# Attention with its two layer normalisations moved from DVE to ACT, and DVE's small work laid out anew

## The reference, cut to what matters

```python
x = x + attention(layernorm(x), ctx)        # x, ctx: (16, 128, 256); 16 heads of 16, causal mask
x = x + ffn(layernorm(x))                   # 256 -> 1024 -> gelu -> 256, block floating point

def layernorm(x):                           # per row of 256
    return (x - mean(x)) / sqrt(var(x) + 1e-5)

def block_quant(v):                         # input of both ffn products, blocks of 32
    e = floor(log2(max(abs(block))))
    return round(block / 2**(e - 3)) * 2**(e - 3)
```

## Time and profile before

| | us |
|---|---|
| median of 3 runs | 251.42 |
| the runs | 248.55 to 251.74 |
| the profiled execution | 250.06 |
| its span, first to last instruction | 248.1 |
| PE, DVE, ACT, POOL busy | 213.2, 205.4, 174.5, 119.4 |

### The profile page before, as it was taken

How to read it: one execution, slowest core, us unless ns; L and a number is a source line. 1 busy time by engine, 2 the same in 40 slices (tenths; PEclk the granted TensorE clock), 3 DMA queues, 4 the chain that set the end, 5 groups by cost and what they waited for, 6 DMA issues and landing times.

```text
span 248.1 us, 6413 instructions
## 1 busy us (share of the span) xinstructions
PE 213.2 (86%) x2072; PEld 158.0 (64%) x2072; DVE 205.4 (83%) x880; ACT 174.5 (70%) x458; POOL 119.4 (48%) x120
## 2 busy tenths in 40 slices
PE   7894997997999979999999999778759849959974
PEld 7673775776776757777777777555327526735753
DVE  4443489899499999899999989897696999999971
ACT  2335887978887867987987998774634734856872
POOL 2610015343962954614524432522634757868892
PEclk9998999998899999999999999988976998997999
DMA  6593662743344243234234234387503102010212
GB/s 210 138 297 64 193 166 48 258 85 68 90 88 81 81 96 75 67 77 96 47 81 85 53 68 96 65 134 133 88 16 74 42 21 60 29 42 24 63 50 80
DMA packets 46576, 22.49 MB, mean 91 GB/s; under 512 B 21700, under 2 KB 46288, under 8 KB 46544
## 3 DMA queue, kind: packets, MB, share of 16 engines
q1 hardware_dynamic: 43472, 19.27, 34.2%
q10 hardware_dynamic: 3072, 2.82, 3.8%
HBM read 7.61 MB, written 2.11 MB: 39 GB/s over the span
## 4 chain that ended last, share of the span: by engine, by line
PE 37%; DVE 27%; SPq 16%; issue 9%; DMA 5%; ACT 2%; POOL 2%; ACTq 1%; DVEq 0%
PE bank L1021 8%; DVE prob L782 7%; SPq L257 4%; SPq L287 4%; PE bank L1128 4%; DVE probT L791 4%; SPq L250 4%; PE s_banks L1192 4%; PE s_banks L1070 4%; PE bank L1222 3%; PE bank L1109 3%; PE s_banks L1086 3%; DMA w_rows<-in_L_xattn_Wq 3%; DVE bank L943 2%; DVE hrn L957 2%
## 5 line engine op out<-in xcount | busy, mean ns | idle before, releaser
L457 ACT ACTIVATE prob<-prob,negm 128x128 f32<-128x128 f32 x256 | 81.0, 390 | 19.0 <-DVE negm L782 18.9
L782 DVE CUSTOM_DVE_ANT_0 prob<-s_banks,mask_f 128x128 f32<-128x128 f32 x256 | 58.8, 286 | 12.6 <-PE s_banks L1070 12.5
L683 POOL TENSOR_TENSOR hq<-hrn,h_mag 128x1024 bf16<-128x1024 f32 (+1 forms) x17 | 31.1, 1832 | 19.0 <-DVE hrn L957 16.4
L1021 PE MATMUL bank<-cT,wT 128*128 128x256 f32 x128 | 33.1, 406 | 0.0
L1070 PE MATMUL s_banks<-KS,QC 16*128 16x128 f32 x512 | 23.3, 296 | 8.7 <-DVE QC L771 3.8
L1070 PEld LDWEIGHTS s_banks<-KS,QC 16*128 16x128 f32 x512 | 17.3, 185 | 17.9 <-issue 16.3
L1021 PEld LDWEIGHTS bank<-cT,wT 128*128 128x128 f32 x128 | 25.5, 210 | 3.3
L517 ACT ACTIVATE s_banks<-s_banks 128x512 f32<-128x512 f32 x32 | 17.8, 580 | 10.3 <-PE s_banks L1192 10.1
L583 POOL TENSOR_TENSOR XQ<-xr,x_mag 128x512 bf16<-128x512 f32 x8 | 8.4, 1048 | 33.9 <-DVE xr L860 33.9
L1086 PE MATMUL s_banks<-ident_f,prob 128*128 128x128 f32 x124 | 20.2, 288 | 4.9 <-DVE negm L782 4.0
L1109 PE MATMUL bank<-probT,V 128*32 128x128 f32 x512 | 20.6, 279 | 3.1 <-DVE probT L791 3.0
(11 more groups left out here) (116 smaller groups left out, 430.2 us busy)
## 6 DMA issues: line engine op xcount, KB each, us to landing
oden<-oT SPq DMA_DIRECT2D x60, 64.0 KB, 2.4
KS<-full SPq DMA_DIRECT2D x32, 64.0 KB, 2.3
VS<-full SPq DMA_DIRECT2D x64, 32.0 KB, 2.0
QS<-full SPq DMA_DIRECT2D x29, 64.0 KB, 2.3
out<-full SPq DMA_DIRECT2D x14, 128.0 KB, 1.7
X<-in_x ACTq DMA_DIRECT2D x1, 1536.0 KB, 7.8
cbuf<-in_ctx SPq DMA_DIRECT2D x6, 256.0 KB, 4.6
fc_rows<-in_L_ffn_w_fc SPq DMA_DIRECT2D x1, 1024.0 KB, 6.1
```

The lines of the kernel that those rows point to most:

```text
L457: ins = nc.scalar.activation(prob[:, k % 4, u, s, :], prob[:, k % 4, u, s, :], ACT.Exp, bias=negm[:, k % 4, u, s:s + 1], scale=-1.0)
L683: nc.gpsimd.tensor_tensor(blocks(hq[par][:, some]), blocks(hrn[par][:, some]), spread(h_mag[par][:, n * nb:(n + 1) * nb], nb), ALU.subtract)\
L782: V.tensor_tensor_reduce(prob[:, k % 4, u, s, :], s_banks[:, 2 * (k % 2) + u, s * P:(s + 1) * P], mask_f[:, :], 1.0, LARGEST, ALU.add, ALU ...
L1021: ins = T.matmul(proj_bank(p, t)[:, c * PT:(c + 1) * PT], wT[:, t, k, c, :], src[:, k, :], start=(k == 0), stop=(k == KC - 1))
```

## The change

The six calls of `norm1` for pairs 2 to 7 and the normalisation of pairs 0 to 4 in `quantise` are done by ACT, as an activation with scale rs and bias -mean * rs, both one value per row. POOL makes that bias: two more operations of 128x2 in each of these `power1` and `power2`. On DVE `stats1` moves from group 2 to group 1, the block maxima from group 1 to group 2, `quantise_rest` from group 2 to group 3. On POOL `round_rows` moves behind `power1` and `queries_apart`. Pairs 0 and 1 of the first, and 5 to 7 of the second normalisation stay on DVE. Left out of the diff below are four new tiles of 128x2 (less1, off_1, less2, off_2) and the semaphores less_1, less_2, shift1 and shift2.

```diff
@@ -477,6 +481,21 @@
                                out_b[:, :].rearrange("p (k j r) -> p j k r", j=NJ, r=RPH))\
                     .then_inc(sm["o_copied"], 1)
 
+            def norm1(p):
+                act.wait_ge(sm["shift1"], p - 1)
+                act.wait_ge(sm["tx_done"], p)
+                for b in range(2):
+                    nc.scalar.activation(xn[:, b, :], X[:, 2 * p + b, :], ACT.Identity, scale=rs1[:, b:b + 1],
+                                         bias=off_1[:, b:b + 1]).then_inc(sm["xn_ready"], 1)
+
+            def norm2(p):
+                act.wait_ge(sm["shift2"], p + 1)
+                if p:
+                    act.wait_ge(sm["round2"], p)
+                for b in range(2):
+                    nc.scalar.activation(xn2[:, b, :], X[:, 2 * p + b, :], ACT.Identity, scale=rs2[:, b:b + 1],
+                                         bias=off_2[:, b:b + 1]).then_inc(sm["xn2_done"], 1)
+
             def step(i, par, first, last):
                 k = 2 * NW * i
                 exps(k)
@@ -492,6 +511,8 @@
                 copy_v(i, par)
                 if not last:
                     copy_proj(i + 1, 1)
+                if i > 2:
+                    norm2(i - 3)
 
                 exps(k + 4)
                 exps(k + 5)
@@ -505,6 +526,7 @@
                 copy_out(i, 0)
                 if ahead(i):
                     copy_tc(i + 2)
+                    norm1(i + 2)
                 if not first and not last:
                     invert(i - 1)
 
@@ -571,11 +593,25 @@
             def power1(p):
 
                 pool.wait_ge(sm["eps1"], p + 1)
+                if p > 1:
+                    nc.gpsimd.tensor_scalar(less1[:, :], mv1[:, :, 0], -1.0, 0.0, ALU.mult, ALU.add)\
+                        .then_inc(sm["less_1"], 1)
                 nc.gpsimd.tensor_tensor(rs1[:, :], ve1[:, :], neg_half[:, :], ALU.pow).then_inc(sm["pow1"], 1)
+                if p > 1:
+                    pool.wait_ge(sm["less_1"], p - 1)
+                    pool.wait_ge(sm["pow1"], p + 1)
+                    nc.gpsimd.tensor_tensor(off_1[:, :], less1[:, :], rs1[:, :], ALU.mult).then_inc(sm["shift1"], 1)
 
             def power2(p):
                 pool.wait_ge(sm["eps2"], p + 1)
+                if p < NPAIR - 3:
+                    nc.gpsimd.tensor_scalar(less2[:, :], mv2[:, :, 0], -1.0, 0.0, ALU.mult, ALU.add)\
+                        .then_inc(sm["less_2"], 1)
                 nc.gpsimd.tensor_tensor(rs2[:, :], ve2[:, :], neg_half[:, :], ALU.pow).then_inc(sm["pow2"], 1)
+                if p < NPAIR - 3:
+                    pool.wait_ge(sm["less_2"], p + 1)
+                    pool.wait_ge(sm["pow2"], p + 1)
+                    nc.gpsimd.tensor_tensor(off_2[:, :], less2[:, :], rs2[:, :], ALU.mult).then_inc(sm["shift2"], 1)
 
             def round_rows(p):
 
@@ -635,13 +671,13 @@
                 if 1 <= i < 4:
                     for u in range(3 * i - 3, min(3 * i, 8)):
                         round_weights(u)
-                if i > 2:
-                    round_rows(i - 3)
                 if ahead(i):
                     power1(i + 2)
                 if not last:
                     queries_apart(i + 1, 1 - par)
-                else:
+                if i > 2:
+                    round_rows(i - 3)
+                if last:
                     normalise(i - 1)
                     power2(i - 2)
 
@@ -835,10 +871,11 @@
 
             def quantise(p):
 
-                dve.wait_ge(sm["pow2"], p + 1)
+                if p >= NPAIR - 3:
+                    dve.wait_ge(sm["pow2"], p + 1)
                 if p >= NPAIR - 2:
                     dve.wait_ge(sm["h_exp_done"], 4 if p == NPAIR - 2 else LAST_OUT + 4)
-                for b in range(2):
+                for b in range(2 if p >= NPAIR - 3 else 0):
                     V.tensor_scalar(normal2(p)[:, b * E:(b + 1) * E], X[:, bass.ds(2 * p + b, 1), :].rearrange("p o e -> p (o e)"),
                                     mv2[:, b, 0:1], rs2[:, b:b + 1], ALU.subtract, ALU.mult)\
                         .then_inc(sm["xn2_done"], 1)
@@ -902,8 +939,8 @@
                 copy_pt(k)
                 maxes(k + 3)
                 copy_pt(k + 1)
-                if i > 2:
-                    quantise(i - 3)
+                if ahead(i):
+                    stats1(i + 2)
                 weights_at(i, 1)
 
                 maxes(k + 4)
@@ -911,9 +948,7 @@
                 maxes(k + 5)
                 copy_pt(k + 3)
                 if i > 2:
-                    quantise_rest(i - 3)
-                if ahead(i):
-                    stats1(i + 2)
+                    quantise(i - 3)
                 weights_at(i, 2)
 
                 if last:
@@ -922,8 +957,8 @@
                 copy_pt(k + 4)
                 maxes(k + 7)
                 copy_pt(k + 5)
-                if ahead(i):
-                    norm1(i + 2)
+                if i > 2:
+                    quantise_rest(i - 3)
                 weights_at(i, 3)
                 if last:
                     stats2(i - 2)
```

More of the change, by code:

```diff
@@ L88, in build_program @@
         rs1 = sb("rs1", [P, 2])
+        less1 = sb("less1", [P, 2])
+        off_1 = sb("off_1", [P, 2])
         xn = sb("xn", [P, 2, E])
@@ L117, in build_program @@
         rs2 = sb("rs2", [P, 2])
+        less2 = sb("less2", [P, 2])
+        off_2 = sb("off_2", [P, 2])
         xn2 = sb("xn2", [P, 2, E])
@@ L142, in build_program @@
         names = """x0_in x1_in x_in c0_in c1_in wq_in wk_in wv_in wp_in bias_in brow_in fc_in pj_in
-            iota v1_set qs_set warm perm_set row_cast col_cast row_bits wT_in wT_out wp_permuted b_parts b_moved ones_set
+            iota v1_set qs_set warm perm_set row_cast col_cast row_bits wT_in wT_out wp_permuted b_parts b_moved ones_set less_1 less_2 shift1 shift2
             bpart_set bn1 ag1 eps1 pow1 xn_ready tx_done tx_copied tc_done tc_copied
```

## The result

The changed kernel takes **254.62 us** (median of 4 runs, 252.23 to 257.98) beside 250.42 us for the kernel before on the same chip (4 runs, 248.55 to 251.74); the ratio is 1.0156, 95% interval 1.009 to 1.0221. Timed again with the second group of experiments it is 1.016 (1.0069 to 1.0251). That is slower by more than nothing; that it is slower by less than 2% is likelier than not but not shown, since both intervals reach past 1.02. Ratios here compare undisturbed runs only and medians are over all runs, so a quotient of two medians can differ from the ratio beside it.

A forecast was written before the change was run, and what follows sets the result against it. PE, DVE's extra work and the loop of SP and ACT were taken as near-equal bounds. Terms 1.28 + 3.38 = 4.7 us gave 254.7 on the profile, 256.1 on the median; forecast 255.4 us, range 251.5 to 259.

The forecast's parts named there:

- slower, by less than 2%: Whole kernel: forecast 255.4 us, a sum just under the 2% (5.0 us) line; chance within 2% 0.52.
- The loop of SP and ACT: SP's transfers and ACT's copy_out: turn grows to 19.83 us, KS issues at 85.41, 105.24, 125.07 and 144.90.
- The pair's price: ACT's normalising pair from SBUF, scale and bias per row: 0.80 us taken, 0.72 and 1.28 kept as ends.
- The gain of steps 3 and 4: DVE's work removed: 1.6 us back in step 3, at most 0.5 us a step over steps 4 to 6.
- The sum, its first term: Step 7 begins 1.63 us late by the copy of QS, 0.35 taken back on DVE: 1.28 us.
- The sum, its second term: Last step: late rounding moves normalise(6) on POOL from 172.88 to 176.26; all 3.38 us goes to the end.
- The statistics in group 1 ...: nothing, at most 0.2: Steps 1 and 2: statistics beside an exponent group of the weights, third group lighter by as much; at most 0.2 us.
- The dear pair: Rival: pair on ACT costs 1.28 us instead of 0.80; sum 6.6 us, 258.0 on the median; chance 0.28.
- The shorter queue: Rival: SP's part of a turn about 12.2 us, turn 18.9, nothing accumulates; sum 1.8 us, 252.5; chance 0.13.
- Not slower: Rival: ACT absorbs the pair, steps 4 to 6 run at PE's 18.38 us; 250.0 to 251.3; chance 0.06.
- The signs: KS issues near 105, 125, 145; PE waiting for xn, steps 4 to 6; DVE's wait before quantise(5) 2 us longer.

The follow-up runs named there:

- Experiments 2: Changed kernel with ACT's norm1 pair ahead of copy_out(i, 0) instead of behind copy_tc; 1.0027 against the kernel before, 250.79 us beside 251.04.
- experiment 5: Changed kernel with two buffers for oT used in turn, norm1 left in place; 1.0027 against the kernel before, 250.25 us beside 251.07.
- experiment 8: Kernel before with two buffers for oT, nothing else; ratio 1.0023, 250.36 us beside 251.57.
- experiment 4: Kernel before with only quantise_rest(4) moved behind the last maxima and copies on DVE; ratio 1.0096, 253.59 us beside 251.04.
- experiment 1: Changed kernel with POOL's normalise(6) and power2(5) ahead of round_rows(4) in the last step; 1.0155 against the kernel before, 253.99 us beside 251.04.
- experiment 10: Changed kernel with two oT buffers, POOL's normalise(6) and power2(5) ahead of round_rows(4), and first three steps' statistics in group 2; 0.9951 against the kernel before, 248.82 us.
- 9: Changed kernel with two oT buffers and POOL's normalise(6) and power2(5) ahead of round_rows(4); 0.9973 against the kernel before, 249.16 us beside 251.57.

## Why the forecast was right, and where it was not

The forecast was 255.4 us, and 254.62 came; "slower, by less than 2%" was the likeliest case, and the measured 1.0156 lies in it, though the interval reaches 1.022. That the change is slower, and by the loop, was foreseen; that the size fits so well is luck, because in the profile both terms of the sum came out otherwise.

**The loop of SP and ACT: right.** KS issues were forecast at 85.41, 105.24, 125.07 and 144.90 and came at 85.77, 104.80, 124.43 and 144.41. Experiments 2 and 5 open the loop in two different ways, and each brings 1.016 to 1.003. PE waits 0.74 us for ACT before the transposes of `xn` in steps 5 and 6, and these steps are 19.6, where 19.8 was forecast. That the loop was as near to being the bound as PE in the kernel before is not borne out: opening it there shows no gain (experiment 8).

**The pair's price: too low.** Taken at 0.80 us from a pair out of PSUM with one bias, measured 0.98 to 0.99. From the Trainium skill (ScalarE: Activation LUTs, What ACT_TABLE_LOAD costs) I had estimated 0.98, and the trace now agrees with it. The near row differs in two things, one operand per row in place of two and PSUM in place of SBUF; no run here separates them.

**The gain of steps 3 and 4: right in kind, larger.** Forecast were 1.6 us in step 3 and up to 0.5 in each steady step; step 3 went from 20.84 to 18.26 and step 4 from 18.87 to 18.26. So the loop bound only from step 5 on, not from step 4.

**The sum, its first term: 1.28 forecast, 0.05 measured.** The forecast let step 7 begin late, by the copy of QS. Step 7 began at 155.74, where it had begun at 155.69. QS was issued 1.14 us later, but its transfers landed 2.4 to 2.7 us after their issue, where one had taken 3.8 before, and POOL's copy began at 154.60 for 154.55; and steps 3 and 4 had won more than was forecast. What the loop costs in step 7 is seen beside experiment 5, where step 7 begins 3.88 us earlier and the rounding comes 1.94 earlier.

**The sum, its second term: 3.38 forecast, 2.11 measured.** `normalise(6)` began at 174.99, where 176.26 was forecast. The chain of the rounding was priced rightly: the add 0.41 after the copies, POOL 0.77 after that, free 1.00 later for 1.15. But the copies let go of DVE at 172.81, not at 173.93, the time taken over from the kernel before. There PE's project of pair 5 (four matmuls of 128x256, twice) took 1.92 and 1.09 us, at a granted clock of 0.58 from 166 to 170; in the changed kernel it took 1.03 twice, at 1.00. The rounding alone, on the kernel before, costs 2.4 us by the runs (experiment 4).

**A delay that the forecast did not have: the inverse.** SP's queue runs without a pause from the KS issue of step 6, 1.14 us late, to the last transfers of `oT` in step 7. Before and with the change:

```profile
163.70 5.85 SPq L287 DMA_DIRECT2D oden<-oT  x8
```

```profile
164.95 5.68 SPq L291 DMA_DIRECT2D oden<-oT  x8
```

ACT's inverse waits for them and starts at 172.62, 1.11 later than before. `normalise(6)` takes the later of inverse and rounding, so this delay is not added: the inverse alone would give 1.03, the rounding gives 2.11.

So by the trace the change costs 2.2 us, by the medians 4.2, and only the latter is near the sum's 4.7. Between the two lies what differs from run to run. The four timed runs of the changed kernel, 252.23, 254.53, 254.72 and 257.98 us, had mean granted clocks of 0.952, 0.938, 0.946 and 0.920, and the first of them is the one in the profile. A second profile of the changed kernel, 257.39 us at a mean granted clock of 0.926 for 0.952, has its first KS issue at 88.50, 2.7 later, ahead of the steps that the loop bounds. What makes the clock fall in one run and not in another was not found.

**"The statistics in group 1 ...: nothing, at most 0.2": wrong.** PE waits 0.90 us in step 1 and 1.81 in step 2 for maxima that stand behind them, and in this profile the matmuls behind the second wait run slow. Time line of PE in step 2, the changed kernel and then experiment 1:

```profile
71.48 1.09 PE L1121 MATMUL s_banks<-ident_f,prob 128*128 128x128 f32 x4 [1.81 <-DVE negm L818]
72.36 2.89 PE L1056 MATMUL bank<-cT,wT 128*128 128x256 f32 x8
```

```profile
72.47 0.63 PE L1122 MATMUL s_banks<-ident_f,prob 128*128 128x128 f32 x4 [1.82 <-DVE negm L819]
72.94 1.89 PE L1057 MATMUL bank<-cT,wT 128*128 128x256 f32 x8
```

The same eight took 1.89 before; from 70 to 76 the granted clock was 0.72 for 1.00, and step 2 is 22.05 us for 20.83. In experiment 1 the same wait was followed by 1.89 us at a granted clock of 1.00, so the wait is the statistics' work (experiment 10 moves them, and most of it goes), but the lower clock does not come with it each time. What the wait is worth in time stays open.

**The rivals.** The dear pair was half right: 0.98 lies between 0.80 and 1.28, but past the 0.9 us from which the rival put the change over 2%, and that is not shown. The shorter queue came in one turn of three: SP's parts were 12.18, 12.79 and 13.13 us, where the rival had 12.2 throughout. "Not slower" gave 18.4 us steps if the turn's part on SP came under 11.7; it never did in the changed kernel, and with two buffers it no longer mattered: 18.26.

**The signs.** KS issues and PE's waits for `xn` came as written, the latter in steps 5 and 6 alone. DVE's wait before `quantise(5)` was 1.1 us longer (3.13 for 2.01), not 2, and ended at 180.11, not near 182.7. DVE was busy 4.6 us less, not 8, and ACT 7.5 more, not 9.

## What to carry to other kernels

Before work is moved to an engine with idle time, follow the loops that run through it: this one had 30% to spare and no room at one place, between a buffer's release and the transfer that refills it. Where two delays end in the same instruction, take the later, not the sum. Here a second buffer, or a place ahead of the wait, took the whole loss away with the same instructions. A time taken over from the kernel before carries the granted clock of that run: here that was 1.1 us of one term.

## What the runs showed of the hardware that was not expected

An activation of 128x256 f32 from SBUF with a scale and a bias per row has a record of 0.59 to 0.61 us. A pair takes 1.10 from the first start to the last end, and the next instruction starts 0.99 after the first; DVE did the pair in 0.73.

A small DVE instruction can stand until an operation of POOL beside it ends. In the profiles before and after, 27 TENSOR_SCALAR records on DVE are over 0.1 us longer than the shortest of their kind; every one of them ends 0.02 to 0.15 us after an operation of POOL. `x_exp` at 135.04 of the changed kernel takes 0.73 us for 0.16, to 135.77, where POOL's copy of QC ends at 135.74. The first `norm2` of step 3 before, 2.35 us for 0.73, from which the forecast took its 1.6 us, is two such records beside POOL's rounding of the weights. Not every overlap does it: `ve` at 174.90 takes 0.17 inside POOL's `XQ`. So an edit of POOL's order alone can lengthen DVE's work, as in experiments 1 and 9.

In the profile of the changed kernel the granted clock fell in two places after PE had stood: at step 2 PE stood 1.81 us, and the eight project matmuls behind it took 2.89 us for 1.89; and after 170 to 174, of which PE worked 1.62 us, the granted clock from 174 to 178 was 0.50 (the 1.2 GHz level). No rule comes out of these runs. The wait of 1.82 us at step 2 was followed by a clock of 1.00 in experiment 1; and PE worked 2.47 us from 162 to 166 before and 2.48 with the change, and ran at 0.58 from 166 to 170 in the one and at 1.00 in the other. Single profiles of one kernel differ here by 2% (252.23 and 257.39).
